# All 1280 columns of the low parts of the exponentials on POOL, none on DVE

## The reference

```
q, k, v = x @ Wq, x @ Wk, x @ Wv                # split into 16 heads of 64
k, v    = one learned null key and null value more for each head
att     = q @ k.T * exp(logit_scale) / 8        # causal; the null key is always seen
y       = softmax(att) @ v
x1      = layernorm(x + y @ Wo)
w, idx  = top 4 of 32 experts, from the best 4 of 8 groups, capacity 640 rows
y_e     = (silu(xe @ w1) * (xe @ w3)) @ w2 * w  # rows gathered for each expert
z       = (silu(x1 @ sw1) * (x1 @ sw3)) @ sw2   # shared expert
out     = layernorm(x1 + sum of y_e + z)
```

## Time and profile before

| | us |
|---|---|
| median of 3 runs | 1114.77 |
| time of the profiled execution | 1128.02 |
| its span, first to last instruction | 1126.3 |
| PE busy | 874.7 |
| DVE busy | 755.2 |
| ACT busy | 664.0 |
| POOL busy | 618.0 |

### The profile page before, as it was taken

The page is one execution under the profiler, slowest core; times in us unless marked ns, Lnnn a source line. Parts: engine busy times, 40 slices in busy tenths (PEclk is TensorE's granted clock), DMA queues, the critical chain, the costliest instruction groups (busy, mean ns, idle before and its releaser), DMA issues.

```text
span 1126.3 us, 25835 instructions
## 1 busy us (share of the span) xinstructions
PE 874.7 (78%) x8987; PEld 647.8 (58%) x8987; DVE 755.2 (67%) x2620; ACT 664.0 (59%) x1267; POOL 618.0 (55%) x526
## 2 busy tenths in 40 slices
PE   5769999999898999999899989865666666676500
PEld 2346676676676766767677767753454555555400
DVE  3557878998998998998998999982532222222127
ACT  4467887886787887888788878751112222222204
POOL 6033434366546557547637636755416666666667
PEclk9889999999999999999999999995867887766755
DMA  5564576543333434343433424004023333333146
GB/s 148 171 226 134 166 212 179 146 127 97 77 91 98 107 72 110 89 95 87 111 86 96 112 61 112 31 9 145 28 87 100 108 110 99 106 105 98 54 179 215
DMA packets 100466, 126.21 MB, mean 112 GB/s; under 512 B 18707, under 2 KB 61162, under 8 KB 99312
## 3 DMA queue, kind: packets, MB, share of 16 engines
q1 hardware_dynamic: 91120, 107.70, 34.9%
q0 software_dynamic: 9216, 16.86, 4.7%
HBM read 33.96 MB, written 42.24 MB: 68 GB/s over the span
## 4 chain that ended last, share of the span: by engine, by line
PE 38%; DVE 23%; issue 11%; another core or an unknown queue 10%; ACT 9%; SPq 4%; DMA 4%; DVEq 0%; ACTq 0%; POOL 0%; POOLq 0%
PE PS L1074 6%; DVE JUNK L1288 4%; PE PS L927 4%; SPq L1723 4%; PE PS L896 3%; PE PS L953 3%; PE PS L950 3%; DMA Q<-QL 3%; ACT PH L1155 2%; PE PS L971 2%; DVE NMD L1306 2%; PE PS L972 2%; DVE PL L1313 2%; PE PS L973 2%
## 5 line engine op out<-in xcount | busy, mean ns | idle before, releaser
L1616 POOL TENSOR_TENSOR PL<-PF,PH 128x1024 f16<-128x1024 f32 x128 | 275.5, 2152 | 329.0 <-ACT PH L1155 321.1
L1288 DVE CUSTOM_DVE_ANT_0 JUNK<-PS,M 128x512 f16<-128x512 f32 (+3 forms) x512 | 237.5, 484 | 59.3 <-PE PS L927 56.4
L1149 ACT ACTIVATE PF<-PS 128x512 f32<-128x512 f32 (+1 forms) x384 | 187.6, 526 | 72.7 <-PE PS L953 61.2
L1649 POOL DMA_INDIRECT y_rows<-BIG,Q x160 | 155.4, 972 | 108.6 <-ACT BIG L1202 63.4
L1155 ACT ACTIVATE PH<-PF 128x1280 f16<-128x1280 f32 x128 | 161.9, 1265 | 0.0
L927 PE MATMUL PS<-K,Q 128*128 128x512 f16 (+3 forms) x512 | 133.2, 306 | 34.1 <-DMA Q<-QL 22.8
L950 PE MATMUL PS<-Q,K 128*128 128x512 f16 (+3 forms) x512 | 150.8, 303 | 5.7 <-ACT PF L1149 5.2
L1640 POOL DMA_INDIRECT xe_rows<-PAY,DEST x128 | 127.8, 998 | 44.6 <-issue 31.5
L953 PE MATMUL PS<-Q,K 128*128 128x512 f16 (+3 forms) x512 | 148.2, 302 | 0.0
L971 PE MATMUL PS<-VH,PH 128*128 128x65 f16 x1280 | 136.6, 195 | 13.5 <-DVE Y L1336 8.2
L973 PE MATMUL PS<-VH,PL 128*128 128x65 f16 x1280 | 136.8, 194 | 0.0
(11 more groups left out here) (214 smaller groups left out, 2059.5 us busy)
## 6 DMA issues: line engine op xcount, KB each, us to landing
K<-KH SPq DMA_DIRECT2D x128, 128.0 KB, 2.4
Q<-QH SPq DMA_DIRECT2D x128, 128.0 KB, 2.4
xe_rows<-PAY SPq DMA_DIRECT2D x20, 520.0 KB, 4.1
Q<-xe_rows SPq DMA_DIRECT2D x32, 325.0 KB
K<-KL SPq DMA_DIRECT2D x64, 128.0 KB, 2.4
Q<-QL SPq DMA_DIRECT2D x64, 128.0 KB, 2.7
y_rows<-PAY SPq DMA_DIRECT2D x16, 512.0 KB, 4.8
K<-in_L_ffn_w_dram SPq DMA_DIRECT2D x96, 64.0 KB
```

The source lines that it names most:

```text
L1149: e.activation(PF[:, n % PBUF, c0:c0 + width], PS[:, k, 0:width], ACT.Exp).then_inc(s["c_exp"], 1)
L1288: e.tensor_tensor_reduce(JUNK[:, n_ttr % 2, 0:width], PS[:, 2 + k, c0:c0 + width], M0[:, 512 - width:512], 1.0, -3e38, ALU.add, ALU.max, M ...
L1616: e.tensor_tensor(PL[:, n % PBUF, PSPLIT:1280], PF[:, n % PBUF, PSPLIT:1280], PH[:, n % PBUF, PSPLIT:1280], ALU.subtract).then_inc(s["c_lp ...
L1649: e.indirect_dma_start(out=y4[:, :], out_offset=bass.IndirectOffsetOnAxis(ap=XE[:, x_ % 6, k, 128:129].bitcast(I32), axis=0), in_=OUT[:, x ...
```

## The change

```diff
-PSPLIT = 256
 ...
     def low_p(n):
         step("low p", n)
-        mark("lc", n, by="c_lc")
         mark("lp", n, by="c_lp")
 ...
             elif name == "values":            # PE
                 w.wait_ge(*at("hc", n))
-                w.wait_ge(*at("lc", n))
                 w.wait_ge(*at("lp", n))
 ...
             elif name == "scores":            # ACT
                 w.wait_ge(*at("hc", n - PBUF))
-                w.wait_ge(*at("lc", n - PBUF))
                 w.wait_ge(*at("lp", n - PBUF))
 ...
-            elif name == "low p":             # DVE
-                n, = a
-                for seg in range(3):
-                    w.wait_ge(*at("exp", n, seg))
-                w.wait_ge(*at("hc", n))
-                w.wait_ge(*at("pv", n - PBUF))
-                e.tensor_tensor(PL[:, n % PBUF, 0:PSPLIT], PF[:, n % PBUF, 0:PSPLIT], PH[:, n % PBUF, 0:PSPLIT],
-                                ALU.subtract).then_inc(s["c_lc"], 1)
 ...
             elif name == "low p":             # POOL, its waits are unchanged
-                e.tensor_tensor(PL[:, n % PBUF, PSPLIT:1280], PF[:, n % PBUF, PSPLIT:1280], PH[:, n % PBUF, PSPLIT:1280],
-                                ALU.subtract).then_inc(s["c_lp"], 1)
+                e.tensor_tensor(PL[:, n % PBUF, :], PF[:, n % PBUF, :], PH[:, n % PBUF, :], ALU.subtract).then_inc(s["c_lp"], 1)
```

More of the change, by code:

```diff
@@ L94, in plan @@
         "c_x", "c_pm", "c_am", "c_dm", "c_st", "c_mx", "c_pj", "c_pv", "c_exp", "c_hc", "c_aj", "c_ttr",
-        "c_lc", "c_lp", "c_dj", "c_dv", "c_dr", "c_y", "c_mrow", "c_xr", "c_pg", "c_xts", "c_sc", "c_fill", "c_ph",
+        "c_lp", "c_dj", "c_dv", "c_dr", "c_y", "c_mrow", "c_xr", "c_pg", "c_xts", "c_sc", "c_fill", "c_ph",
         "c_pz", "c_as", "c_dz")}
```

## The result

| | before | after |
|---|---|---|
| median of 20 runs each, us | 1118.32 | 1121.82 |
| lowest to highest | 1113.92 to 1124.35 | 1116.70 to 1126.30 |
| ratio of after to before, 95% interval | | 1.0032, 1.0016 to 1.0047 |
| profiled execution / its span | 1128.02 / 1126.3 | 1120.91 / 1119.1 |

The change makes the kernel slower by 0.32%, some 3.5 us. The prediction said 1108, 7 us faster than before. The two profiles tell it the other way round, since the one of before is of an execution 10 us above the median.

A forecast was written before the change was run, and what follows sets the result against it. The prediction held that only the attention could move, with DVE and PE handing the path to each other and no engine bounding alone. Its terms, -21 + 21 - 15 + 8 = -7 us, gave 1108 us, range 1088 to 1130.

The forecast's parts named there:

- the later PL: POOL's low parts in the attention: ending 0.5 us later costs nothing; without cover, 0.5 us a head, 64 us in all.
- its estimate of 2.77 us: POOL's 1280-column subtraction by the Trainium skill's rate, about 2.6 cycles of 1.2 GHz an element; the forecast took 2.57 to 2.67.
- (a): DVE in the attention: removing L1313 takes its share off the chain of waits, a gain of 21 us.
- (c): DVE in the attention: reaching NMD, R and others earlier, some slip in before POOL's hold, a gain of 15 us.
- (b): DVE steps standing behind POOL in the attention: thirty stands each last 0.5 us longer, a cost of 21 us.
- (d): DVE steps newly caught behind POOL's end or no longer shielded by L1313, a cost of 8 us.
- Rival 3: Attention: longer hold catches MM and NMD more often, DVE, ACT and PE stand together; slower by 14 us, 1129; chance 0.34.
- its mark of 1.1 us: Mean of NMD on DVE over its 32 passes, 974 ns before; passing about 1.1 us decides for the slower case.
- Rival 1: Attention: DVE's load decides, not single steps; net 60 us less load cuts PE's waits by 27 us, time 1088; chance 0.12.
- Rival 2: Attention: the wait only moves, POOL holding what L1313 kept behind it; terms cancel, time 1114 to 1117; chance 0.16.

The follow-up runs named there:

- e1: Kernel before without DVE's low parts, POOL kept at 1024 columns, columns 0 to 255 left zero: 0.9885 and, again, 0.9841 of before.
- e11: Kernel before with DVE's 256 columns kept but POOL forming only the last 16, columns 256 to 1263 zero: 0.9562 of before.
- e14: The changed kernel, unaltered, timed and profiled again beside the kernel before: 1.0036 of before.
- e4: The changed kernel with NMD issued right behind NG, about 1 us earlier on DVE: 0.9984 of before.
- e9: The changed kernel with one single-input reduction forming the negated maxima in place of MM and NG, NMD right behind: 0.9948 of before.
- e5: The changed kernel with POOL forming only the last 16 columns, DVE none, the other 1264 zero: 0.9575 of before.
- e2: Kernel before with POOL forming all 1280 columns and DVE still forming its 256 into an unread tile: 1.0426 of before.
- the five parts: The changed kernel with POOL's one operation of 1280 columns cut into five of 256, semaphore on the last: 0.9826 of before.
- e13: Kernel before with 512 low-part columns on DVE in place of 256, and 768 on POOL in one operation: 0.9832 of before.

## Why the prediction was wrong, by its own steps

**Right: the bound and the mechanism.** Only the attention moved; before's second profile and e1, on like chips, have the same 327 us from the start of the last "high p" on. DVE stands still while POOL subtracts, POOL's instruction grew by 0.49 us, and the later PL is hidden. In the earlier trace rows the prediction took DVE's wait (L1321) as one for PL; it is for PE's values product, and nothing hangs on it. Its remark that both rows lie lower than the rate behind its estimate of 2.77 us is not so for the 512-column row: that rate gives 1.11 us there, and the row has 1.256.

**(a), the removal, 21 us on the path:** e1 shows 12 to 17 for (a) and (c) together, where the prediction had 36. By (a) alone the chain had named about the right size. e11 suggests that it is standing and not work: without the hold L1313's 52 us of bare work are free.

**(b), longer stands, 21 us, with (d), 8 us for those newly caught:** e1 to after shows 12 to 21 together, 2 to 5 of which can be PE's clock, a term that the prediction did not have. Right in kind, too high.

**(c), the step that failed, 15 us of gain:** it held that DVE, with less ahead of it, would slip NMD and R in before POOL. In e1, where only the removal acts, NMD's stands went up, to 37 and 36 us from 19 and 28 in the two profiles of before, and 19 of the 32 NMD started inside a hold in place of 10 and 14. Of the three whose means the prediction named, R alone escaped (8 and 5 us before, 1.1 in e1, 1.5 after). NMD got no lead over POOL. In the third unit of the third to the seventh batch it started 0.01 us ahead of POOL in the first profile of before and had slipped in already (in the second, three of these five did); in e1 it starts 0.14 to 0.17 us behind POOL's start and stands for 2.0 us. The four others newly caught in e1 had started 3.3 us behind POOL, when the hold was over, and meet it now. Unit 14, DVE and POOL, first in before, then in e1:

```profile
353.47 0.17 DVE L1306 TENSOR_TENSOR NMD<-NG,NS 128x16 f32<-128x16 f16 x1
353.48 2.17 POOL L1616 TENSOR_TENSOR PL<-PF,PH 128x1024 f16<-128x1024 f32 x1 [1.31 <-ACT PH L1155]
```
```profile
339.52 2.00 DVE L1305 TENSOR_TENSOR NMD<-NG,NS 128x16 f32<-128x16 f16 x1
339.36 2.12 POOL L1608 TENSOR_TENSOR PL<-PF,PH 128x1024 f16<-128x1024 f32 x1
```

So PH, and with it POOL, moved forward at least as far as DVE did, the case to which the step had given half. At the longer hold it varies: in e14 the same unit starts 0.33 us ahead of POOL and slips in. In the changed kernel 18, 17 and 13 of the 32 NMD stood (three profiles), against 11 and 15 before. All stands other than L1313's rose from 76 and 83 to 96 us in e1, and to 108 after. Without (c) the sum of the prediction is -21 + 21 + 8 = +8, against 3.5 measured; that it comes near is partly luck, as (a), (b) and (d) were all too high.

**The rivals.** Rival 3 had the sign and the sight of it: NMD's mean passed its mark of 1.1 us, though the second profile of before was already at 1.26, and MM stayed under its 0.8 (0.88 in e14). Its size, +14, was four times too large. e4 and e9 each took about 30 of the row maximum's 54 us of stands and moved 0.15% and 0.5 to 0.9%, so it is a part of the cost; how large a part isn't settled, as neither freed all of it. The layer norm's and the gate's steps that read only SBUF (X, EQ, DF) stand as well, 43 us of the 108. Rival 1 fell with the result: PE's wait for the maxima's bank did fall, from 16.7 to 13.2 us, and DVE got 41 us free, and the kernel is no faster for it. Rival 2, no change, and with it the rule of the Trainium skill (Perfetto Trace Analysis, Optimizing Scalar/DVE Operations) that moving work between these two might not help, came within 0.3%, by the cancellation that it names.

**Open.** How much of the loss falls on which stand isn't resolved: stands and time go together only roughly (82 us of stands had 0.998, 96 us had 0.984 to 0.989). PE's clock is a rival of the same size as the net loss: the changed kernel stands 27 to 34 us at half clock in the attention, before 23 and 24, which costs up to 2 to 5 us of matmul work. No run separates it from the stands; PE is less busy ahead of such a stretch, so it may well be a consequence of them. In e1, e5 and e11 part of the low parts is zero. That the zeros themselves change no time was not tested alone; e2, the five parts and e13, which form all of them, point the same way. That ACT and PE wait for NMD is in the trace; that their waits and no others make up the 3.5 us isn't shown. e2's 45 us for 0.49 us more hold are measured, but why they are over twice what the change paid for the same growth is only argued: L1313's own stands rose from 52 to 83 us with it.

## What to carry to other kernels

When one engine's instruction can hold another's, busy time is no measure of load: compare the minimum of a line with its mean, and price the removal of an instruction by the stand it makes as well as by its work. Moving columns to the engine that holds lengthens every hold; here shortening the hold by giving the other engine more work gained 1.7%, as did cutting the operation into five, though a held instruction can still stand through several parts, and at ten parts the fixed cost made the result late. A step taken out of an in-order queue shifts everything behind it against the other engine's starts, and whether that meets or misses them has to be read from both engines' start times, not assumed as a gain. Where PE waits, look at its granted clock behind the wait too.

## What the runs showed of the hardware that was not expected

DVE is sometimes held before the profile shows POOL's subtraction as started. In the changed kernel NMD starts at 234.67 and ends at 237.93; POOL is still in an indirect DMA until 235.24, and its subtraction is recorded from 235.25 to 237.89. First DVE, then POOL:

```profile
234.67 3.26 DVE L1302 TENSOR_TENSOR NMD<-NG,NS 128x16 f32<-128x16 f16 x1
```
```profile
234.26 0.98 POOL L1627 DMA_INDIRECT xe_rows<-PAY,DEST  x1 [0.30 <-issue]
235.25 2.64 POOL L1604 TENSOR_TENSOR PL<-PF,PH 128x1280 f16<-128x1280 f32 x1
```

That is 0.58 us ahead of POOL's start; six DVE steps of this profile began 0.2 to 0.7 us ahead of a subtraction and ended only behind it. The indirect DMAs alone don't do it: in e5 and e11, with all their scatters, the stands are 2 to 3 us in all. So either a hold is longer than the instruction that the profile shows, or the recorded start of POOL's instruction is late; which of the two isn't shown.

POOL's subtraction has a fixed part: 128 columns take 0.43 us, 256 0.67, 512 1.16, 1024 2.13, 1280 2.62, that is about 0.19 us and 1.90 ns a column. The prediction's line through an operation of another type had 0.38 us and 1.71 ns.
